# Local transformer stage: the score block directly ahead of the first mixture on TensorE, the row maxima behind the last rotation on VectorE

## The chip, the cores and the metric

The kernel runs on one core of one Trainium2 chip. The metric is the device time of one execution in microseconds (us); lower is better. The engines are TensorE (PE, with its weight loads as PEld), VectorE (DVE), ScalarE (ACT), GpSimd (POOL) and SyncE (SP), which only issues transfers here.

## The reference, cut to what matters

The whole network is four pairs of an attention branch `s` and a gate branch `g`, each joined by `x = x + s * silu(g)`. The change touches one branch only, the first gate: a local transformer of six layers over 16 sequences of 256 tokens with 16 heads of 64.

```python
def attn_layer(x, Wqkv, qs, ksc, Wo):
    q, k, v = (sh(t) for t in jnp.split(x @ Wqkv, 3, -1))
    q, k = l2norm(q) * qs, l2norm(k) * ksc
    q = q * cos * scale + rotate_half(q) * sin * scale
    k = k * cos / scale + rotate_half(k) * sin / scale
    # windows of 32 queries see their own 32 keys and the 32 before
    sim = jnp.einsum('bhwie,bhwje->bhwij', bq, bk2) * QK_SCALE
    sim = jnp.where(mask, -jnp.finfo(sim.dtype).max, sim)
    out = jnp.einsum('bhwij,bhwje->bhwie', jax.nn.softmax(sim, -1), bv2)
    return out.reshape(b, n, INNER) @ Wo
for i in range(6):
    x = attn_layer(shift_tokens(x), ...) + x
    x = ffn_layer(shift_tokens(x), ...) + x     # layer norm, two products, gelu gate
```

## The kernel before

The stage works on 192 tiles (six layers of 32 tiles of 128 tokens). It is a software pipeline written out by hand: `for n in range(LAST_STEP)` stands in the program of every engine, and in step n an engine does for tile n, n-1, n-2, n-3 and n-4 what falls to it. Each engine runs its own instructions strictly in the order written; semaphores tie them together. So what matters is which block stands where in a step. `now(lag)` is true where tile n - lag exists.

TensorE's blocks in a step, in their order before the change, with the names used below:

- P0, q0, P1, q1, O0, k0, O1, k1, P2: `project(n, unit)` (L1123, 128x512, units 0 to 3), `turn_qk(n - 2, ...)` (L1131, four transposes each) and `project_out(n - 4, part)` (L1186, parts O0 to O3)
- p0: `turn_probs(n - 3, 0)` (L1159, four transposes)
- S: `scores(n - 2)`, the mask as eight small products (L1142) and 128 passes of 64x64 (L1150)
- P3, p1 (the second half of `turn_probs`), O2
- every fourth step `turn_rows` (L1215); in two steps of a layer `turn_values`
- M0: `mix(n - 3, 0)` (L1174), the first half of probabilities times values
- in a step that is a multiple of four `hidden` (L1224) between the next blocks; in odd steps `turn_x` (L1113)
- O3, then M1: `mix(n - 3, 1)`

The two mixtures share the PSUM banks `u_bank`. M1 may overwrite nothing that ScalarE has not copied out:

```python
def mix(i, piece):
    pe.wait_ge(sem["copied"], copied_at["p", i, 1])
    if piece == 1 or i >= 1:
        pe.wait_ge(sem["u_copied"], 4 * i + 2 * piece)
```

ScalarE's order in a step, which the change leaves alone, ends as follows. The exponentials of tile n-2 stand ahead of the copy of the first mixture of tile n-3:

```python
    square(n, 3)
    copy_turned("p", n - 3, 1)
    exps(n - 2, 0); exps(n - 2, 1)              # L1336, wait for "shifted"
    copy_rows(...)                              # every fourth step, L1365
    copy_mixed(n - 3, 0)                        # L1344, sets "u_copied"
    copy_x(...); gelu(..., 0); gelu(..., 1)     # in some steps
    copy_mixed(n - 3, 1)
```

VectorE rotates the four projected units (`rotate`, three instructions each: L1507, L1511 and the sum of squares L1515), and in `shift_scores(n - 2)` takes the row maxima of the scores (L1522, two instructions, wait for "scored") and subtracts them (L1527, two instructions, set "shifted"). In one step of four `measure_rows` stands between `rotate(n, 1)` and `rotate(n, 2)`. The next step begins with `sum_probs` (L1534). GpSimd adds and normalises what was rotated, and divides the probabilities by their sums.

Of the kernel before, what the change touches and what calls it, by code (L numbers as in the profile page):

```python
# [885 lines left out]
def local_transformer_stage(core):  # L886
# [10 lines left out]
    with ExitStack() as ctx:  # L897
# [43 lines left out]
        def group_at(n, lag):  # L941
            q = (n - lag) // GROUP
            return q if (n - lag) % GROUP == 0 and 0 <= q < GROUPS else None

        def starts(n, at):
            return n // NT if n % NT == at and n < TILES else None
# [50 lines left out]
        def wait_turn_bank(pe, *key):  # L997
            k = turn_number[key]
            if k > 0:
                name, count = turn_free[k - 1]  # L1000
                pe.wait_ge(sem[name], count)

        def ring(*key):
            return ring_bank[ring_number[key] % 2]
# [7 lines left out]
        with nc.Block() as block:  # L1012
# [93 lines left out]
            def _(pe):  # L1106
# [28 lines left out]
                def scores(i):  # L1135
                    b, t = i // TPB, i % TPB
                    pe.wait_ge(sem["copied"], copied_at["k", i, 1])
                    if i >= 1:
                        pe.wait_ge(sem["shifted"], 2 * i)
                    for w in range(WPT):  # L1140
                        for h in range(2):
                            nc.tensor.matmul(score_bank[h][32 * w:32 * w + 32, :], core.pick[64 * h:64 * h + 64, :],  # L1142
                                             core.window_mask[64 * h:64 * h + 64, int(t == 0 and w == 0), :], start=True, stop=False,
                                             skip_group_check=True)
                    for j in range(PAIRS):
                        for w in range(WPT):
                            at = WINDOW * (WPT * t + w)
                            for h in range(2):
                                rows_h = slice(64 * h, 64 * h + 64)
                                last = nc.tensor.matmul(score_bank[h][32 * w:32 * w + 32, 64 * j:64 * j + 64],  # L1150
                                                        qt[rows_h, i % 2, j, 32 * w:32 * w + 32], kt[rows_h, b % 2, j, at:at + 2 * WINDOW],
                                                        start=False, stop=True, skip_group_check=True)
                    last.then_inc(sem["scored"], 1)
# [37 lines left out]
                def turn_values(l, half):  # L1191
                    pe.wait_ge(wvo_in, 32 * (l + 1))
                    wait_turn_bank(pe, "v", l, half)
                    for j in range(4):
                        at = (4 * half + j) * P
                        last = nc.tensor.transpose(turn_bank[:, j * P:(j + 1) * P], wv[:, at:at + P], core.ident[:, :])
                    last.then_inc(sem["turned"], 1)
# [41 lines left out]
                for n in range(LAST_STEP):  # L1239
                    now = lambda lag: 0 <= n - lag < TILES  # L1240
                    if now(0):
                        project(n, 0)
                    if now(2):
                        turn_qk(n - 2, "q", 0)
                    if now(0):
                        project(n, 1)
                    if now(2):
                        turn_qk(n - 2, "q", 1)
                    if now(4):
                        project_out(n - 4, 0)  # L1250
                    if now(2):
                        turn_qk(n - 2, "k", 0)
                    if now(4):
                        project_out(n - 4, 1)
                    if now(2):
                        turn_qk(n - 2, "k", 1)
                    if now(0):
                        project(n, 2)
                    if now(3):
                        turn_probs(n - 3, 0)  # L1260
                    if now(2):
                        scores(n - 2)
                    if now(0):
                        project(n, 3)
                    if now(3):
                        turn_probs(n - 3, 1)
                    if now(4):
                        project_out(n - 4, 2)
                    if group_at(n, 11) is not None:
                        turn_rows(group_at(n, 11))  # L1270
                    for half in range(2):
                        if starts(n, 1 + half) is not None:
                            turn_values(n // NT, half)
                    if now(3):
                        mix(n - 3, 0)
                    if group_at(n, 12) is not None:
                        hidden(group_at(n, 12), 0)
                    if n % 2 == 1 and n + 1 < TILES:
                        turn_x((n + 1) // 2)
                    if now(4):  # L1280
                        project_out(n - 4, 3)
                    if group_at(n, 12) is not None:
                        hidden(group_at(n, 12), 1)
                    if now(3):
                        mix(n - 3, 1)
                    if starts(n, 3) is not None:
                        multiply_weights(n // NT)
                    if group_at(n, 12) is not None:
                        hidden(group_at(n, 12), 2)
                    if group_at(n, 13) is not None:  # L1290
                        project_hidden(group_at(n, 13))
# [203 lines left out]
            def _(dve):  # L1495
                def rotate(i, unit):
                    g, t, which = UNITS * i + unit, i % TPB, unit // 2
                    if i % NT == 0 and unit % 2 == 0:
                        dve.wait_ge(rope_in[which], 16 * (i // NT + 1))
                    dve.wait_ge(sem["squared"], g + 1)  # L1500
                    if i >= 3:
                        wait_turned(dve, "qk"[which], i - 3, unit % 2)
                    if g >= 2:
                        dve.wait_ge(sem["added"], g - 1)
                    src = ring("p", i, unit)
                    cos = rope[:, which, t, 0, :].rearrange("p (a d) -> p a d", a=1).to_broadcast([P, 8, DH])
                    nc.vector.tensor_tensor(a[:, g % (3 * UNITS), :].rearrange("p (h d) -> p h d", d=DH), src.rearrange("p (h d) -> p h d", d=DH),  # L1507
                                            cos, ALU.mult)
                    halves = src.rearrange("p (h s d) -> p h s d", s=2, d=32)[:, :, ::-1, :]
                    sin = rope[:, which, t, 1, :].rearrange("p (a s d) -> p a s d", a=1, s=2).to_broadcast([P, 8, 2, 32])  # L1510
                    nc.vector.tensor_tensor(b_[:, g % 2, :].rearrange("p (h s d) -> p h s d", s=2, d=32), halves, sin,  # L1511
                                            ALU.mult).then_inc(sem["rotated"], 1)
                    if i >= 2 and unit == 0:
                        dve.wait_ge(sem["rn_ready"], i - 1)
                    nc.vector.tensor_reduce(n2[:, i % 2, 8 * unit:8 * unit + 8], sq[:, g % 2, :].rearrange("p (h d) -> p h d", d=DH), AX.X,  # L1515
                                            ALU.add).then_inc(sem["summed"], 1)
# [74 lines left out]
                for n in range(LAST_STEP):  # L1591
                    now = lambda lag: 0 <= n - lag < TILES
                    if now(3):
                        sum_probs(n - 3)
                    if now(5):
                        store(n - 5)
                    if group_at(n, 11) is not None:
                        normalise_rows_of(group_at(n, 11))
                    if now(0):
                        rotate(n, 0)  # L1600
                        rotate(n, 1)
                    if group_at(n, 9) is not None:
                        measure_rows(group_at(n, 9))
                    if now(0):
                        rotate(n, 2)
                    if now(2):
                        shift_scores(n - 2)
                    if now(0):
                        rotate(n, 3)
                    if group_at(n, 12) is not None:  # L1610
                        gate_hidden(group_at(n, 12))
                    if group_at(n, 13) is not None:
                        store_group(group_at(n, 13))
# [1286 lines left out]
```

## Time and profile before

| | |
|---|---|
| time, median of three runs | 5806.92 us (5806.7 to 5816.7) |
| time of the profiled execution | 5807.41 us |
| span of the profile | 5805.6 us |
| busy over the whole span | PE 83%, DVE 66%, PEld 58%, ACT 49%, POOL 44% |
| instructions | 144393 |
| busiest lines of the changed stage | POOL L1435 976.7 us, PE L1123 828.0 us, PE L1186 823.6 us |

The profiled time and the span differ by 1.8 us, the part outside the first and last instruction. The stage in question lies between about 219 and 3616 us of the span and takes well over half of it; the rest of the program is the same in both kernels. "Idle before, releaser" says how long an engine stood still ahead of a group and whose work ended that.

### The profile page before, as it was taken

Reading aid. Unit: us, or ns where it says so; the run is one execution under the profiler, and the core shown is the slowest. Engines: PE = TensorE matmul, PEld = TensorE weight load, DVE = VectorE, ACT = ScalarE, POOL = GpSimd, SP = SyncE. Lnnn points to the kernel's source line nnn. Section 1 sums busy time; section 2 is a strip of 40 time slices with the busy share of each in tenths; the row PEclk is TensorE's granted clock in tenths of the full one; section 3 lists DMA queues with packets and bytes.
Section 4 is the critical chain, followed back from the end, with each engine's and each line's share of the span. In section 5 each row is a group of like instructions: output and inputs, shape, how many; then the busy total and the mean of one; then the engine's idle time right before and its main releaser. Section 6 shows DMA issues by size and latency. Waiting matters only on the chain. (4 is left out here: it accounts for less than half of the span.)

```text
span 5805.6 us, 144393 instructions
## 1 busy us (share of the span) xinstructions
PE 4827.4 (83%) x57263; PEld 3362.5 (58%) x57263; DVE 3834.8 (66%) x9149; ACT 2866.4 (49%) x6252; POOL 2569.4 (44%) x3065
## 2 busy tenths in 40 slices
PE   7699999999999999999999998533689996067874
PEld 3366666666666666666666666323556664045653
DVE  7677777777777777777777775666367777633421
ACT  2266665666666666666666655200256664322331
POOL 4476666766777677667766765012200000000000
PEclk9899999999999999999999999765889998587987
DMA  0211111111111111111111100011100000001001
GB/s 20 67 31 24 25 33 35 24 25 39 31 24 33 31 28 24 33 34 27 24 33 23 26 20 13 21 41 55 31 18 2 2 2 3 20 5 27 25 21 39
DMA packets 312161, 150.56 MB, mean 26 GB/s; under 512 B 146143, under 2 KB 301003, under 8 KB 311243
## 3 DMA queue, kind: packets, MB, share of 16 engines
q1 hardware_dynamic: 309451, 137.20, 9.8%
q8 instruction: 457, 7.49, 0.5%
q0 software_dynamic: 2048, 4.20, 0.3%
q14 instruction: 205, 1.68, 0.1%
HBM read 101.10 MB, written 27.41 MB: 22 GB/s over the span
## 5 line engine op out<-in xcount | busy, mean ns | idle before, releaser
L1435 POOL TENSOR_TENSOR loc_a<-loc_a,loc_b 128x512 f32<-128x512 f32 x768 | 976.7, 1274 | 231.6 <-DVE loc_b L1511 231.0
L1123 PE MATMUL psum<-loc_wqk,loc_xt 128*128 128x512 f32 x1536 | 828.0, 621 | 19.0 <-issue 8.3
L1186 PE MATMUL psum<-loc_m,xn_rows 128*128 128x128 f32 x6144 | 823.6, 277 | 3.9 <-DVE y_rows L1543 2.6
L1307 ACT ACTIVATE loc_sq<-psum 128x512 f32<-128x512 f32 x768 | 455.1, 593 | 680.6 <-PE psum L1123 680.0
L1460 POOL TENSOR_TENSOR loc_a<-loc_a,loc_rn 128x512 f32<-128x512 f32 x768 | 785.4, 1045 | 0.1
L1186 PEld LDWEIGHTS psum<-loc_m,xn_rows 128*128 128x128 f32 x6144 | 754.1, 193 | 45.6 <-issue 42.6
L1507 DVE TENSOR_TENSOR loc_a<-psum,loc_rope 128x512 f32<-128x512 f32 x768 | 523.4, 681 | 334.8 <-ACT loc_sq L1307 322.5
L1467 POOL TENSOR_TENSOR xn_cols<-xn_cols,loc_rec 128x512 f32<-128x512 f32 x384 | 394.5, 1048 | 687.2 <-DVE loc_rec L1538 687.1
L1344 ACT COPY xn_rows<-psum 128x512 f32<-128x512 f32 x768 | 411.7, 588 | 221.6 <-PE psum L1174 217.6
L1511 DVE TENSOR_TENSOR loc_b<-psum,loc_rope 128x512 f32<-128x512 f32 x768 | 520.7, 678 | 0.0
L1515 DVE TENSOR_REDUCE loc_n<-loc_sq 128x8 f32<-128x512 f32 x768 | 517.1, 673 | 0.0
L1131 PEld LDWEIGHTS psum<-ident,loc_a 128*128 128x128 f32 x3072 | 338.9, 141 | 275.1 <-issue 262.3
L1131 PE MATMUL psum<-ident,loc_a 128*128 128x128 f32 x3072 | 478.1, 278 | 13.4 <-ACT loc_qt L1325 7.2
L1174 PE MATMUL psum<-xn_cols,loc_x 64*128 64x256 f32 x3072 | 437.8, 402 | 19.9 <-ACT xn_rows L1344 19.2
L1325 ACT COPY loc_kt<-psum 128x512 f32<-128x512 f32 x384 | 224.7, 585 | 312.5 <-PE psum L1131 312.5
L1150 PE MATMUL psum<-loc_kt,loc_qt 64*32 64x64 f32 x24576 | 293.1, 225 | 72.7 <-issue 72.6
L1174 PEld LDWEIGHTS psum<-xn_cols,loc_x 64*128 64x128 f32 x3072 | 273.4, 187 | 115.5 <-issue 80.0
L1150 PEld LDWEIGHTS psum<-loc_kt,loc_qt 64*32 64x32 f32 x24576 | 281.9, 105 | 88.5 <-issue 78.2
L364 POOL TENSOR_TENSOR s_rows<-s_rows,l2a_gamma 128x1024 f32<-128x1024 f32 x2 | 4.9, 2445 | 717.5 <-DVE s_rows L293 717.5
L1159 PEld LDWEIGHTS psum<-ident,xn_cols 128*128 128x128 f32 x1536 | 177.8, 141 | 238.8 <-issue 238.6
L1224 PE MATMUL psum<-x_rows,loc_w 128*128 128x512 f32 (+1 forms) x576 | 287.8, 623 | 18.3 <-ACT x_rows L1375 17.4
L1123 PEld LDWEIGHTS psum<-loc_wqk,loc_xt 128*128 128x128 f32 x1536 | 232.3, 190 | 113.1 <-issue 52.2
(365 smaller groups left out, 8819.5 us busy)
## 6 DMA issues: line engine op xcount, KB each, us to landing
loc_x<-loc_shifted SPq DMA_DIRECT2D x192, 256.0 KB, 4.0
loc_shifted<-y_rows SPq DMA_DIRECT2D x144, 64.0 KB
loc_wqk<-in_L_ffn_Wqkv SPq DMA_DIRECT2D x24, 256.0 KB, 3.7
x_rows<-y_rows SPq DMA_DIRECT2D x96, 64.0 KB
x_rows<-y_rows SPq DMA_DIRECT2D x96, 63.5 KB
moe_w<-in_L_ffn_W SPq DMA_DIRECT2D x16, 256.0 KB, 4.6
l3a_qk<-l3a_rot SPq DMA_DIRECT2D x16, 256.0 KB, 2.1
grp_w<-in_L_ffn_W SPq DMA_DIRECT2D x16, 256.0 KB, 2.8
```

The lines of the kernel that those rows point to most:

```text
L1123: nc.tensor.matmul(ring("p", i, unit), xt[:, b % 2, t * P:(t + 1) * P], wqk[:, unit * 512:(unit + 1) * 512], start=True, stop=True).then_i ...
L1131: last = nc.tensor.transpose(turn_bank[:, j * P:(j + 1) * P], a[:, (UNITS * i + unit) % (3 * UNITS), j * P:(j + 1) * P], core.ident[:, :])
L1150: last = nc.tensor.matmul(score_bank[h][32 * w:32 * w + 32, 64 * j:64 * j + 64], qt[rows_h, i % 2, j, 32 * w:32 * w + 32], kt[rows_h, b % ...
L1174: last = nc.tensor.matmul(u_bank[h][:, 256 * v:256 * v + 256], x2[rows_h, b % 3, WPT * t + w, :], pt[rows_h, i % 2, :, 32 * w:32 * w + 32] ...
L1186: last = nc.tensor.matmul(y_bank[:, 0:P], u[:, i % 2, h // 2, h % 2, :], m[:, h, :], start=(h == 0), stop=(h == HEADS - 1))
L1307: nc.scalar.activation(sq[:, g % 2, :], ring("p", i, unit), ACT.Square).then_inc(sem["squared"], 1)
L1344: nc.scalar.copy(to, u_bank[h].rearrange("p (w j q) -> p w j q", w=2, j=PAIRS)).then_inc(sem["u_copied"], 1)
L1435: nc.gpsimd.tensor_tensor(part, part, b_[:, g % 2, :], ALU.add).then_inc(sem["added"], 1)
L1460: nc.gpsimd.tensor_tensor(part, part, rn[:, i % 2, 8 * unit:8 * unit + 8].rearrange("p (h e) -> p h e", e=1).to_broadcast([P, 8, DH]), ALU ...
L1507: nc.vector.tensor_tensor(a[:, g % (3 * UNITS), :].rearrange("p (h d) -> p h d", d=DH), src.rearrange("p (h d) -> p h d", d=DH), cos, ALU. ...
L1511: nc.vector.tensor_tensor(b_[:, g % 2, :].rearrange("p (h s d) -> p h s d", s=2, d=32), halves, sin, ALU.mult).then_inc(sem["rotated"], 1)
L1515: nc.vector.tensor_reduce(n2[:, i % 2, 8 * unit:8 * unit + 8], sq[:, g % 2, :].rearrange("p (h d) -> p h d", d=DH), AX.X, ALU.add).then_in ...
```

## The change

On TensorE, `scores(n - 2)` moves from its place between p0 and P3 to a place behind P3, p1, O2 and the two occasional turns, directly ahead of M0. On VectorE, `shift_scores(n - 2)` moves from ahead of `rotate(n, 3)` to behind it. No instruction is added or removed, and ScalarE, GpSimd and SyncE keep their order.

```diff
@@ TensorE @@
                         turn_probs(n - 3, 0)
-                    if now(2):
-                        scores(n - 2)
                     if now(0):
                         project(n, 3)
...
                         if starts(n, 1 + half) is not None:
                             turn_values(n // NT, half)
+                    if now(2):
+                        scores(n - 2)
                     if now(3):
                         mix(n - 3, 0)
@@ VectorE @@
                     if now(0):
                         rotate(n, 2)
+                        rotate(n, 3)
                     if now(2):
                         shift_scores(n - 2)
-                    if now(0):
-                        rotate(n, 3)
```

TensorE's blocks from p0 to M1 in a plain step of the steady state (p0 is the first L1159 row, S the rows L1142 and L1150, P3 is L1123, M0 and M1 are L1174), before:

```order
L1159 MATMUL psum<-ident,xn_cols 128x128 x4
L1142 MATMUL psum<-loc_window_mask,loc_pick 32x512 x8
L1150 MATMUL psum<-loc_kt,loc_qt 32x64 x64
L1123 MATMUL psum<-loc_wqk,loc_xt 128x512
L1159 MATMUL psum<-ident,xn_cols 128x128 x4
L1186 MATMUL psum<-loc_m,xn_rows 128x128 x4
L1174 MATMUL psum<-xn_cols,loc_x 128x256 x4
L1186 MATMUL psum<-loc_m,xn_rows 128x128 x4
L1174 MATMUL psum<-xn_cols,loc_x 128x256 x4
```

The same blocks on TensorE in the changed kernel:

```order
L1159 MATMUL psum<-ident,xn_cols 128x128 x4
L1123 MATMUL psum<-loc_wqk,loc_xt 128x512
L1159 MATMUL psum<-ident,xn_cols 128x128 x4
L1186 MATMUL psum<-loc_m,xn_rows 128x128 x4
L1142 MATMUL psum<-loc_window_mask,loc_pick 32x512 x8
L1150 MATMUL psum<-loc_kt,loc_qt 32x64 x64
L1174 MATMUL psum<-xn_cols,loc_x 128x256 x4
L1186 MATMUL psum<-loc_m,xn_rows 128x128 x4
L1174 MATMUL psum<-xn_cols,loc_x 128x256 x4
```

S went down past three blocks; between S and M1 there were five blocks, and now there are two.

VectorE in the same step, from the third rotation to the sums of the next step, before:

```order
L1507 TENSOR_TENSOR loc_a<-psum,loc_rope 128x512
L1511 TENSOR_TENSOR loc_b<-psum,loc_rope 128x512
L1515 TENSOR_REDUCE loc_n<-loc_sq 128x8
L1522 TENSOR_REDUCE loc_top<-psum 128x8 x2
L1527 TENSOR_TENSOR xn_cols<-psum,loc_top 128x8x64 x2
L1507 TENSOR_TENSOR loc_a<-psum,loc_rope 128x512
L1511 TENSOR_TENSOR loc_b<-psum,loc_rope 128x512
L1515 TENSOR_REDUCE loc_n<-loc_sq 128x8
L1534 TENSOR_REDUCE loc_total<-xn_cols 128x8 x2
```

And VectorE in the changed kernel, at the same place:

```order
L1507 TENSOR_TENSOR loc_a<-psum,loc_rope 128x512
L1511 TENSOR_TENSOR loc_b<-psum,loc_rope 128x512
L1515 TENSOR_REDUCE loc_n<-loc_sq 128x8
L1507 TENSOR_TENSOR loc_a<-psum,loc_rope 128x512
L1511 TENSOR_TENSOR loc_b<-psum,loc_rope 128x512
L1515 TENSOR_REDUCE loc_n<-loc_sq 128x8
L1522 TENSOR_REDUCE loc_top<-psum 128x8 x2
L1527 TENSOR_TENSOR xn_cols<-psum,loc_top 128x8x64 x2
L1534 TENSOR_REDUCE loc_total<-xn_cols 128x8 x2
```

The maxima and the subtraction (L1522, L1527) stand one rotation later, directly ahead of the sums of the next step.

## Rows read from the trace of the kernel before

**Rows 1.** Busy time in one stretch of the stage; us, PE, PEld, DVE, ACT, POOL, PEclk, DMA:

```profile
core 0: us, PE busy (x) PEld busy (x) DVE busy (x) ACT busy (x) POOL busy (x), PEclk, DMA share, GB/s
2000.00:3000.00 1000.00, 964.01 (x13141) 683.34 (x13139) 751.21 (x1394) 616.18 (x1182) 707.52 (x866) 1.00 0.13 30
```

**Rows 2.** TensorE's waits, 600 to 3400 us; us in total, times, longest:

```profile
PE psum L1150 <- issue: 56.0, 39, 2.1
PE psum L1174 <- ACT xn_rows L1344: 14.9, 64, 0.3
```

**Rows 3.** Timeline of TensorE, plain step, p0 to M1; start, us, operation:

```profile
2004.82 0.63 PE L1159 MATMUL psum<-ident,xn_cols 128*128 128x128 f32 x4
2005.38 0.41 PE L1142 MATMUL psum<-loc_window_mask,loc_pick 64*32 64x512 bf16 x8
2005.60 1.46 PE L1150 MATMUL psum<-loc_kt,loc_qt 64*32 64x64 f32 x128
2006.99 1.13 PE L1123 MATMUL psum<-loc_wqk,loc_xt 128*128 128x512 f32 x2
2007.95 0.60 PE L1159 MATMUL psum<-ident,xn_cols 128*128 128x128 f32 x4
2008.39 1.06 PE L1186 MATMUL psum<-loc_m,xn_rows 128*128 128x128 f32 x8
2009.38 1.13 PE L1174 MATMUL psum<-xn_cols,loc_x 64*128 64x256 f32 x8
2010.44 1.16 PE L1186 MATMUL psum<-loc_m,xn_rows 128*128 128x128 f32 x8
2011.78 1.14 PE L1174 MATMUL psum<-xn_cols,loc_x 64*128 64x256 f32 x8 [0.18 <-ACT xn_rows L1344]
```

**Rows 4.** Timeline of VectorE and ScalarE, the same step:

```profile
2007.37 1.28 DVE L1522 TENSOR_REDUCE loc_top<-psum 128x8 f32<-128x512 f32 x2
...
2009.28 1.23 ACT L1336 ACTIVATE xn_cols<-xn_cols 128x512 f32<-128x512 f32 x2
...
2009.76 0.68 DVE L1507 TENSOR_TENSOR loc_a<-psum,loc_rope 128x512 f32<-128x512 f32 x1
...
2010.56 1.07 ACT L1344 COPY xn_rows<-psum 128x512 f32<-128x512 f32 x2
...
2011.55 1.27 DVE L1534 TENSOR_REDUCE loc_total<-xn_cols 128x8 f32<-128x512 f32 x2
```

**Rows 5.** Timeline of TensorE in a step with turned rows (L1215):

```profile
2023.96 0.63 PE L1215 MATMUL psum<-ident,loc_rows 128*128 128x128 f32 x4
2024.52 1.13 PE L1174 MATMUL psum<-xn_cols,loc_x 64*128 64x256 f32 x8
2025.91 0.41 PE L1113 MATMUL psum<-ident,y_rows 128*128 128x128 f32 x2 [0.26 <-ACT x_rows L1365]
```

**Rows 6.** Timeline of VectorE in a step with measured rows:

```profile
2127.83 1.27 DVE L1522 TENSOR_REDUCE loc_top<-psum 128x8 f32<-128x512 f32 x2
```

**Rows 7.** Timeline of TensorE in a step with hidden products (L1224):

```profile
2113.27 2.01 PE L1224 MATMUL psum<-x_rows,loc_w 128*128 128x512 f32 x4 [0.37 <-ACT x_rows L1375]
```

**Rows 8.** Timeline of TensorE around three stalls in the score block:

```profile
519.82 0.24 PE L1150 MATMUL psum<-loc_kt,loc_qt 64*32 64x64 f32 x1 [1.84 <-issue]
...
905.19 0.45 PE L1150 MATMUL psum<-loc_kt,loc_qt 64*32 64x64 f32 x29 [2.05 <-issue]
...
1228.42 0.34 PE L1150 MATMUL psum<-loc_kt,loc_qt 64*32 64x64 f32 x13 [1.86 <-issue]
1228.69 1.13 PE L1123 MATMUL psum<-loc_wqk,loc_xt 128*128 128x512 f32 x2
...
1235.08 1.14 PE L1174 MATMUL psum<-xn_cols,loc_x 64*128 64x256 f32 x8 [0.18 <-ACT xn_rows L1344]
```

**Rows 9.** Busy time and PEclk in the stretches behind those three stalls:

```profile
520.00:523.40 3.40, 3.40 (x23) 2.41 (x22) 3.30 (x6) 2.12 (x4) 2.72 (x3) 1.00 0.03 7
...
905.80:909.00 3.20, 3.20 (x10) 2.06 (x10) 3.20 (x6) 1.16 (x3) 0.45 (x1) 0.50 0.02 5
1230.10:1233.30 3.20, 3.20 (x16) 2.80 (x16) 3.20 (x7) 1.96 (x4) 2.02 (x3) 0.50 0.01 3
```

## The prediction

> **What bounds the kernel now.** I read the busy time of the stage first, then TensorE's waits, then the timeline of one step on three engines. In a thousand microseconds of the stage TensorE is busy for 964, at a granted clock of 1.00 (2.4 GHz), while VectorE, ScalarE and GpSimd have 25% to 38% to spare [rows 1]. So TensorE's stream is the bound: what makes it stand still is paid, unless it stands still later anyway. Its waits are few. The largest is "issue" inside the score block S, 39 times, 56.0 us; the next is the second mixture M1 on ScalarE's copies of the first one, 14.9 us in 64 steps, at most 0.3 us each [rows 2].
>
> That second entry is small but decides the case. In the plain step M1 starts at 2011.78 with a wait whose releaser is the copy L1344 [rows 3], and the copy ran from 2010.56 for 1.07, to 2011.63 [rows 4]. So M1 starts 0.15 behind the end of the copy: it has no slack against it. What holds the copy? ScalarE's two exponentials start at 2009.28 and take 1.23, to 2010.51, and the copy stands 0.05 behind them; M0 itself ends at 2009.38 + 1.13 = 2010.51 as well [rows 3, 4]. Both releases fall together: the reader should see a chain with zero slack that runs S, maxima (2007.37), exponentials (2009.28), copy (2010.56), M1 (2011.78). From the start of the maxima to M1 it takes 4.41 us [rows 3, 4]. The program's order puts the exponentials of tile n-2 ahead of the copy of tile n-3, so the copy inherits every delay of S, though its data have nothing to do with it.
>
> **What the change does, plain step.** S has 1.61 us to the next block and ends 1.68 behind its start (2005.60 + 1.46 - 2005.38). In the new order, from p0 at 2004.82: P3 may follow after 0.44 (as O2 follows p1, 2007.95 to 2008.39), at 2005.26; p1 after 0.96, at 2006.22; O2 at 2006.66; S after 0.99, at 2007.65; M0 after 1.61, at 2009.26 instead of 2009.38; S ends at 2009.33 [rows 3]. VectorE is no obstacle: the maxima's old place at 2007.37 goes to the fourth rotation, which takes 1.79 (2009.76 to 2011.55), so VectorE is free at 2009.16 [rows 4]. The maxima start on the end of S, about 2009.36, which is **1.99 us** later than before. With the same 4.41 us M1 starts at 2013.77, against 2011.78. TensorE has only O3 to hide that: M0 takes 1.06 to the next block, O3 starts at 2010.32 and ends 1.16 later, at 2011.48 [rows 3]. TensorE then stands still for **2.29 us** in every plain step.
>
> Nothing later gives that back. TensorE's next waits are small [rows 2], and P0, q0 and the rest follow M1 back to back. The fourth rotation is earlier, but TensorE did not wait for it. GpSimd gets the sums' reciprocals later by less than TensorE is delayed. The 0.12 us by which M0 is earlier is lost in the wait.
>
> **The other steps, four kinds in turn.**
> - Turned rows: S now also stands behind L1215, which takes 0.56 to the next block [rows 5]. `turn_x` (L1113) waits for ScalarE's L1365, which stands behind the exponentials, already 0.26 now [rows 5]. Everything moves by 1.99 + 0.56 = 2.55 us.
> - Measured rows: VectorE was late, with the maxima at 2127.83 [rows 6] directly behind its third rotation; one rotation more makes it +1.79 us, and S is ready by then.
> - Hidden products: the second hidden block waits for a gelu (L1375), 0.37 now [rows 7], and the gelus stand behind the same copy of M0; +1.99 us.
> - Plain: +1.99 us.
>
> The mean is 2.08 us. 191 steps have both an S and a mixture (192 tiles, one step apart), so the wait costs 397 us. In 12 steps (two a layer) `turn_values` is put ahead of S too, at the same 0.56: 7 us. Together **404 us**. I bound it by 1.9 and 2.25 us a step, 363 to 430 us.
>
> **The clock.** A stall of TensorE can cost more than its length. The stalls inside S are the nearest rows [rows 8]. Behind the one of 2.05 us and the one of 1.86 us the granted clock is 0.50 (1.2 GHz); behind the one of 1.84 us it stays 1.00 [rows 9]. In the second of them P3 to M1 takes 1235.08 - 1228.69 = 6.39 us [rows 8] where the plain step takes 2011.78 - 2006.99 = 4.79 [rows 3]: a fall costs 1.60 us on the path. The new gaps of 2.3 us and more are longer than each of these, and they come in every step. By these rows alone all would be followed by a fall (1.60 x 191 = 306 us); that equal stalls near 1.85 us go either way says that chance has a part, and heavy blocks, not S, stand beside the new gap. I take 0.7, and 0.4 and 1.0 as ends: 0.7 x 1.60 x 191 = **214 us**, between 122 and 306.
>
> The Trainium skill speaks against this term: "TensorE: Matmul & The Clock Gate", section "Why this matters for your kernels", warns only of gaps longer than the ones worked out here. By it the clock would hold and the sum would be 6211. The rows behind the stalls contradict it, so it is a rival only.
>
> **Sum.** 5807.4 (the profiled execution's own time, 0.5 above the median of the runs) + 404 + 214 = 6425 us.
>
> **The rivals.**
> - The wait without the falls. For it: busy blocks on both sides of the gap, and one stall of 1.84 us that was harmless [rows 9]. Against it: two shorter gaps with a fall. 5807 + 404 = 6211 us. Chance 0.08.
> - The stalls inside S go. The 56.0 us of "issue" in 2800 us [rows 2] may be TensorE outrunning the supply of its instructions, and with a pause in each step the supply could keep up. Over the 3400 us of the stage 68 us would be saved: 6357 us. Against it: S itself runs as fast as before. Chance 0.10.
> - The low clock keeps itself up: a fall on every step and half again as many more in the steps with longer gaps. 404 + 2 x 306 = 1016, 6823 us at its worst, from 6560 on. Chance 0.06.
> - Not slower. If M0's own end, and not the exponentials, set ScalarE's copy, M1 would keep its place: M0 even starts 0.12 us earlier (2009.26), giving 191 x 0.12 = 23 us, 5784 us. The two releases do coincide at 2010.51. It decides at maxima that start no later than 2007.37; but S cannot have ended by then in the new order, and ScalarE's order is fixed. Chance 0.02.
> - My forecast, wait and falls: 0.74.
>
> **How the numbers follow.** The predicted time is that of the forecast, 6425. Its own ends are 5807 + 363 + 122 = 6292 and 5807 + 430 + 306 = 6543. The range 6300 to 6545 holds it and the rival without stalls, and leaves out the other three, 0.16, and little more. Faster by over 0.2% (about what a measurement of this kernel can tell from no change) is the last rival, 0.02; within 0.2% would need a near-exact cancellation, 0.01; slower 0.97.
>
> **What the profile after would show.** TensorE's waits: L1174 on ScalarE L1344 as the first entry, some 2.3 us at a time in plain steps, where it was 0.3 at most, and L1113 on L1365 near 2.9 us in the steps with turned rows. The timeline: maxima directly behind the end of S, 4.41 us from maxima to M1. The stage's granted clock below 1.00: with 0.7 falls a step some 0.94, if each lasts a little over the 3.2 us shown at 0.50 [rows 9] in a step of some 20 us. A granted clock of 1.00 would refute the second term; M1 waits of under 1 us would refute the first. VectorE's and ScalarE's busy times should not change. The prediction goes wrong if the exponentials start before S ends plus 1.9 us, or if the falls come less often than four in ten steps.

## The result, and the profile after

The changed kernel takes 6368.71 us (median of four runs, 6363.59 to 6391.32), the kernel before 5811.81 us beside it (5806.7 to 5817.54). The ratio is 1.0965, 95% interval 1.0946 to 1.0984: slower by a tenth. The profiled execution took 6364.08 us with a span of 6362.3 us.

From the page of the changed kernel, busy time and TensorE's granted clock in 40 slices:

```profile
PE 4997.7 (79%) x57229; PEld 3461.3 (54%) x57263; DVE 3871.3 (61%) x9149; ACT 2874.0 (45%) x6252; POOL 2561.5 (40%) x3065
...
PEclk9899999999999999999999999986588999676987
```

VectorE, ScalarE and GpSimd are busy for as long as before, within 37 us. TensorE is busy for 170 us more (4827.4 before) with the same work: part of its work ran slower. The stage alone shows it, in the columns of [rows 1], before and after:

```profile
281.00:3600.00 3319.00, 3176.27 (x43068) 2251.24 (x43074) 2455.77 (x4557) 2030.12 (x3893) 2315.38 (x2831) 1.00 0.12 28
```

```profile
280.00:4147.00 3867.00, 3350.19 (x43017) 2348.47 (x43016) 2487.61 (x4544) 2034.60 (x3889) 2305.06 (x2828) 0.94 0.10 24
```

With all but the same instructions TensorE is busy for 174 us more and idle for 374 us more (517 against 143), together 548 of the 557 us. A mean of 0.94 between 1.0 and 0.5 is (1 - 0.94) x 2 x 3867 = some 460 us at the low clock. TensorE's waits in the stage, in the form of [rows 2], before:

```profile
PE psum L1150 <- issue: 71.5, 49, 2.1
PE psum L1174 <- ACT xn_rows L1344: 18.1, 78, 0.7
PE psum L1224 <- ACT x_rows L1375: 17.4, 46, 0.9
...
PE psum L1113 <- ACT x_rows L1365: 7.2, 28, 0.5
```

And after:

```profile
PE psum L1174 <- ACT xn_rows L1344: 199.9, 93, 2.8
PE psum L1113 <- ACT x_rows L1365: 128.6, 45, 3.1
PE psum L1224 <- ACT x_rows L1375: 107.5, 46, 2.4
PE psum L1150 <- issue: 46.3, 60, 2.1
```

The second mixture's wait for the copy of the first is now at the top, and the two waits of the other step kinds, for ScalarE's instructions behind the exponentials, follow. Together the three are 436 us, where they were 43. The stalls inside the score block went the other way, from 71.5 us in the whole stage to 46.3.

A plain step of the changed kernel on TensorE, from p0 to the block behind M1, to be laid beside [rows 3]:

```profile
2535.68 0.63 PE L1159 MATMUL psum<-ident,xn_cols 128*128 128x128 f32 x4
2536.15 1.02 PE L1123 MATMUL psum<-loc_wqk,loc_xt 128*128 128x512 f32 x2
...
2538.53 0.41 PE L1142 MATMUL psum<-loc_window_mask,loc_pick 64*32 64x512 bf16 x8
2538.75 1.46 PE L1150 MATMUL psum<-loc_kt,loc_qt 64*32 64x64 f32 x128
2540.14 1.13 PE L1174 MATMUL psum<-xn_cols,loc_x 64*128 64x256 f32 x8
2541.20 1.16 PE L1186 MATMUL psum<-loc_m,xn_rows 128*128 128x128 f32 x8
2544.62 2.08 PE L1174 MATMUL psum<-xn_cols,loc_x 64*128 64x256 f32 x8 [2.26 <-ACT xn_rows L1344]
2546.63 1.72 PE L1123 MATMUL psum<-loc_wqk,loc_xt 128*128 128x512 f32 x2
```

VectorE in the same step, from the fourth rotation to the subtraction, beside [rows 4]:

```profile
2538.58 0.69 DVE L1507 TENSOR_TENSOR loc_a<-psum,loc_rope 128x512 f32<-128x512 f32 x1 [0.26 <-POOL loc_a L1435]
...
2540.38 1.28 DVE L1522 TENSOR_REDUCE loc_top<-psum 128x8 f32<-128x512 f32 x2
```

And ScalarE, the exponentials and the copy behind them:

```profile
2542.29 1.23 ACT L1336 ACTIVATE xn_cols<-xn_cols 128x512 f32<-128x512 f32 x2 [3.96 <-DVE xn_cols L1527]
2543.43 1.05 ACT L1344 COPY xn_rows<-psum 128x512 f32<-128x512 f32 x2
```

From p0 the score block starts at 2.85 us (worked out: 2.83), M0 at 4.46 (4.44), the maxima at 4.70 (4.54) and M1 at 8.94 (8.95). M0 ended at 2541.27, and the copy of its result begins at 2543.43: its data lay ready for 2.16 us while ScalarE waited for maxima of another tile. TensorE stands still for 2.26 us (2.29). Behind the pause M1 takes 2.01 us to the next block, where [rows 3] has M0 with 1.06. The clock in the stretches ahead of, behind and after that pause:

```profile
2520.00:2544.40 24.40, 20.15 (x312) 15.51 (x294) 16.64 (x30) 11.85 (x24) 16.49 (x20) 1.00 0.08 18
2544.60:2547.80 3.20, 3.18 (x10) 1.91 (x11) 2.72 (x5) 1.06 (x2) 2.04 (x2) 0.50 0.00 0
2548.00:2560.00 12.00, 11.88 (x203) 8.66 (x201) 8.49 (x14) 5.84 (x12) 9.81 (x12) 1.00 0.22 47
```

The granted clock falls to 1.2 GHz as the pause ends and is back at 2.4 GHz some three microseconds later, after M1 and most of P0 ran slowly. Not every pause has this behind it: counted in the trace between the first and the last score block, 49 of the 106 pauses of 2.1 to 2.4 us were followed by a fall, and 33 of the 44 of 2.8 to 3.2 us. In the step with turned rows the pause is longer, 2.93 us ahead of L1113 (0.26 in [rows 5]):

```profile
2323.84 0.41 PE L1113 MATMUL psum<-ident,y_rows 128*128 128x128 f32 x2 [2.93 <-ACT x_rows L1365]
```

### The profile page after: what moved, and what is told of

Same layout as the page of the kernel before. It is cut to its first block and busy times, and to the rows that moved or that the text cites. A ratio compares the mean times of both kernels' runs of the same rounds, so it can differ in the third digit from the quotient of the medians.

```text
span 6362.3 us, 144359 instructions
## 1 busy us (share of the span) xinstructions
PE 4997.7 (79%) x57229; PEld 3461.3 (54%) x57263; DVE 3871.3 (61%) x9149; ACT 2874.0 (45%) x6252; POOL 2561.5 (40%) x3065
## 5 line engine op out<-in xcount | busy, mean ns | idle before, releaser
L1435 POOL TENSOR_TENSOR loc_a<-loc_a,loc_b 128x512 f32<-128x512 f32 x768 | 970.5, 1276 | 45.3 <-DVE loc_b L1511 45.2
L1123 PE MATMUL psum<-loc_wqk,loc_xt 128*128 128x512 f32 x1536 | 859.5, 643 | 10.3 <-ACT loc_m L1356 4.6
L1186 PE MATMUL psum<-loc_m,xn_rows 128*128 128x128 f32 x6144 | 850.8, 283 | 5.0 <-DVE y_rows L1543 2.6
L1186 PEld LDWEIGHTS psum<-loc_m,xn_rows 128*128 128x128 f32 x6144 | 780.1, 198 | 47.1 <-issue 44.3
L1174 PE MATMUL psum<-xn_cols,loc_x 64*128 64x256 f32 x3072 | 499.6, 445 | 210.8 <-ACT xn_rows L1344 205.1
L1336 ACT ACTIVATE xn_cols<-xn_cols 128x512 f32<-128x512 f32 x384 | 235.6, 630 | 839.8 <-DVE xn_cols L1527 839.8
L1511 DVE TENSOR_TENSOR loc_b<-psum,loc_rope 128x512 f32<-128x512 f32 x768 | 522.4, 680 | 0.0
L1131 PEld LDWEIGHTS psum<-ident,loc_a 128*128 128x128 f32 x3072 | 352.5, 145 | 305.9 <-issue 291.9
L1131 PE MATMUL psum<-ident,loc_a 128*128 128x128 f32 x3072 | 488.1, 283 | 14.7 <-ACT loc_qt L1325 7.1
L1174 PEld LDWEIGHTS psum<-xn_cols,loc_x 64*128 64x128 f32 x3072 | 307.0, 209 | 324.2 <-issue 284.7
L1224 PE MATMUL psum<-x_rows,loc_w 128*128 128x512 f32 (+1 forms) x576 | 312.9, 670 | 108.4 <-ACT x_rows L1375 107.5
L1576 DVE SCALAR_TENSOR_TENSOR x_rows<-psum,loc_b,x_rows 128x512 f32<-128x512 f32 x144 | 107.9, 750 | 372.7 <-PE psum L1224 199.9
L1150 PE MATMUL psum<-loc_kt,loc_qt 64*32 64x64 f32 x24576 | 294.3, 224 | 48.0 <-issue 48.0
L1150 PEld LDWEIGHTS psum<-loc_kt,loc_qt 64*32 64x32 f32 x24576 | 281.5, 105 | 67.4 <-issue 57.1
L1522 DVE TENSOR_REDUCE loc_top<-psum 128x8 f32<-128x512 f32 x384 | 246.7, 684 | 115.3 <-PE psum L1150 110.4
```

Of the source, the lines that this page charges most:

```text
L1123: nc.tensor.matmul(ring("p", i, unit), xt[:, b % 2, t * P:(t + 1) * P], wqk[:, unit * 512:(unit + 1) * 512], start=True, stop=True).then_i ...
L1174: last = nc.tensor.matmul(u_bank[h][:, 256 * v:256 * v + 256], x2[rows_h, b % 3, WPT * t + w, :], pt[rows_h, i % 2, :, 32 * w:32 * w + 32] ...
L1186: last = nc.tensor.matmul(y_bank[:, 0:P], u[:, i % 2, h // 2, h % 2, :], m[:, h, :], start=(h == 0), stop=(h == HEADS - 1))
L1435: nc.gpsimd.tensor_tensor(part, part, b_[:, g % 2, :], ALU.add).then_inc(sem["added"], 1)
```

## The experiments

The account to be tested has two terms: the exponentials ahead of the copy on ScalarE carry every delay of the score block into M1 (wait), and the pauses lower TensorE's clock (falls). Rivals: VectorE's new order is what costs; the wait belongs to the data; the low clock costs nothing on the path. All ratios are to the kernel before on the same chip, whose medians there were 5823 to 5826 us; it was 5811.81 us beside the changed kernel, so differences of some ten microseconds between versions timed on different chips say little.

**E1, the TensorE half alone.** The score block in its new place, VectorE as before.

```diff
                         rotate(n, 2)
-                        rotate(n, 3)
                     if now(2):
                         shift_scores(n - 2)
+                    if now(0):
+                        rotate(n, 3)
```

> The TensorE half of the change alone: the score block directly ahead of the first mixture, VectorE's maxima in their old place ahead of the fourth rotation. Theory (the maxima start on the end of the score block, the exponentials and the copy of the first mixture follow it, and the second mixture waits for that copy): as slow as the changed kernel, 6345 to 6375 us, since VectorE's order was no obstacle in the plain step; only in the one step of four with measured rows may the maxima start some 0.3 us earlier, 48 times, 14 us. Rival (the slowdown comes from VectorE's new order): near 5810 us.

Measured: 6343.7 us, ratio 1.0903 (1.0873 to 1.0933). The TensorE half makes nearly the whole loss: 520 us over the kernel before beside it, where the whole change has 557. Some 36 us are left for the rotation of 1.79 us that the whole change puts ahead of the maxima, more than the 14 expected, but little beside the 342 us that 191 rotations take. E1's first waits differ from the changed kernel's in one:

```profile
PE psum L1174 <- ACT xn_rows L1344: 189.7, 93, 2.8
PE psum L1113 <- ACT x_rows L1365: 127.4, 45, 3.1
PE psum L1224 <- DVE loc_b L1511: 74.6, 45, 1.7
```

With the rotation behind the maxima, the hidden products wait for the fourth rotation (loc_b, L1511) to free their bank.

**E2, the VectorE half alone.** TensorE as before, the maxima behind the fourth rotation.

```diff
                         rotate(n, 2)
+                        rotate(n, 3)
                     if now(2):
                         shift_scores(n - 2)
-                    if now(0):
-                        rotate(n, 3)
```

> The VectorE half alone: TensorE in its old order, the maxima behind the fourth rotation. Theory: the rotation (1.79 us) stands between the third rotation and the maxima, the copy and the second mixture are late by the same 1.79 us in every step, 191 x 1.79 = 342 us, and the gaps make some falls of the clock, 100 to 200 us: 6250 to 6350 us. Rival (the maxima have slack, since their place in the new kernel costs nothing): under 5900 us.

Measured: 6726.78 us, ratio 1.1552 (1.1529 to 1.1576), far above what I expected, and worse than the whole change. VectorE in a plain step of E2, from the third rotation's last instruction to the maxima:

```profile
2488.80 0.68 DVE L1515 TENSOR_REDUCE loc_n<-loc_sq 128x8 f32<-128x512 f32 x1
2490.80 0.69 DVE L1507 TENSOR_TENSOR loc_a<-psum,loc_rope 128x512 f32<-128x512 f32 x1 [1.32 <-ACT loc_sq L1307]
...
2492.61 1.27 DVE L1522 TENSOR_REDUCE loc_top<-psum 128x8 f32<-128x512 f32 x2
```

TensorE in the same step, P3 and M1:

```profile
2489.01 1.13 PE L1123 MATMUL psum<-loc_wqk,loc_xt 128*128 128x512 f32 x2
...
2496.84 1.22 PE L1174 MATMUL psum<-xn_cols,loc_x 64*128 64x256 f32 x4 [3.22 <-ACT xn_rows L1344]
```

The fourth rotation needs P3 and its square, and in the old TensorE order P3 stands behind the score block. VectorE idles 1.32 us for it, and the maxima, whose scores have long been there, idle behind it: they start at 2492.61, 3.1 us behind the end of the third rotation at 2489.48, where in the step of [rows 4] they followed it at once. Counted from the start of the score block (L1142 at 2487.40) they are at 5.21 us instead of 1.99, so 3.22 us late and not 1.79. TensorE's busy time grew by 347 us (5174.8 against 4827.4), where I had 100 to 200 for the clock. 3.22 x 191 + 347 = 962 is close to the 939 us between the two spans (6744.3 and 5805.6). The miss was mine, since I had taken the rotation's duration and not what it waits for.

**E3, the copy ahead of the exponentials.** The changed kernel with one edit on ScalarE.

```diff
-                    if now(2):
-                        exps(n - 2, 0)
-                        exps(n - 2, 1)
...
                     if now(3):
                         copy_mixed(n - 3, 0)
+                    if now(2):
+                        exps(n - 2, 0)
+                        exps(n - 2, 1)
```

> The changed kernel with one more edit, on ScalarE: the copy of the first mixture stands ahead of the exponentials instead of behind them. Theory: the second mixture then waits for nothing but the first mixture and its copy; the 2.0 to 2.5 us go away in plain, measured and turned-rows steps, and the clock stays at 1.00. In the steps with hidden products the gelus now stand behind 1.2 us of exponentials, so those keep some 1.1 us of loss, 48 times, 53 us, while the steps with turned rows win some 0.4 us, 20 us: 5800 to 5860 us. Rival (the wait belongs to the data, or the low clock would stay without the gap): over 6100 us.

Measured: 5836.64 us, ratio 1.0023 (1.0011 to 1.0034). The loss is gone but for 13 us. E3's first waits of TensorE:

```profile
PE psum L1224 <- ACT x_rows L1375: 65.1, 46, 1.4
PE psum L1150 <- issue: 58.5, 66, 2.1
PE psum L1123 <- ACT loc_xt L1300: 17.9, 39, 0.5
...
PE psum L1174 <- ACT xn_rows L1344: 8.5, 48, 0.2
```

M1's wait fell from 199.9 to 8.5 us. What is left is where it was expected, in the gelus of the hidden steps (L1375), which now stand behind the exponentials. The copy of x (L1300), made in odd steps, is a new, small wait of the projections.

**E4, the pause filled.** The changed kernel with products whose results are thrown away, where TensorE would stand still.

```diff
+                def fill(n, count):
+                    if n % 4:
+                        pe.wait_ge(sem["rotated"], UNITS * (n + 1))
+                    to = ring("p", n, 3) if n % 4 else turn_bank
+                    for _ in range(count):
+                        nc.tensor.matmul(to[:, 0:P], core.ident[:, :], core.ident[:, :], start=True, stop=True,
+                                         skip_group_check=True)
...
+                    if now(3) and now(0) and n % 4 == 3:
+                        fill(n, 10)
                     if n % 2 == 1 and n + 1 < TILES:
                         turn_x((n + 1) // 2)
                     if now(4):
                         project_out(n - 4, 3)
+                    if now(3) and now(0) and n % 4 != 3:
+                        fill(n, 6 if n % 4 == 1 else 8)
```

> The changed kernel with products of the identity with itself (128x128, results thrown away, nothing of the computation left out) in TensorE's pause: 8 behind the third part of the output product, 6 in steps with measured rows, 10 ahead of the turn of x in steps with turned rows. They take about as long as the pause, so the wait itself stays. Theory with two terms (wait 404 us, falls of the clock the rest): the granted clock of the stage goes back to nearly 1.00 and the time falls by the clock's part, 150 to 210 us, to 6160 to 6230 us. Rival (the low clock costs nothing on the path, the wait is all): 6360 us or more, since the products can only add.

Measured: 6197.11 us, ratio 1.0645 (1.0623 to 1.0667). Some 1500 products more, and 172 us less than the changed kernel. E4's stage:

```profile
280.00:3975.00 3695.00, 3499.42 (x46010) 2569.39 (x46011) 2483.67 (x4543) 2027.40 (x3883) 2306.77 (x2828) 1.00 0.11 25
```

The granted clock is 1.00 again. The loss against the kernel before beside it is 374 us (6197.11 - 5823.3) instead of 557, so the falls make some 183 us (172 by the medians as they stand, which come from two chips). The 374 us are an upper bound of the wait, since the products may add a little of their own. The split of the stage of the changed kernel says the same without any filling: 174 us more busy, 374 us more idle.

**E5, a small dose.** The score block down past P3 alone, VectorE as before.

```diff
-                    if now(2):
-                        scores(n - 2)
                     if now(0):
                         project(n, 3)
+                    if now(2):
+                        scores(n - 2)
                     if now(3):
                         turn_probs(n - 3, 1)
```

> A small dose: the score block goes down past P3 alone (p0, P3, scores, p1, O2, M0), the maxima stay ahead of the fourth rotation. Theory (no slack at all between the maxima and the second mixture): the score block ends 0.96 - 0.1 us later, the maxima start 0.6 us later in plain, hidden and turned-rows steps and 0.1 us later in steps with measured rows, mean 0.47; 191 x 0.47 = 90 us over the kernel before on the same chip, ratio 1.013 to 1.018, and gaps of under 1 us leave the clock at 1.00. Rival (there is some slack, and only a long delay costs): ratio under 1.003.

Measured: 5860.34 us, ratio 1.0053 (1.0035 to 1.0072), 31 to 34 us. There is a loss at the smallest step down, but a third of the one I expected. E5's waits and stage:

```profile
PE psum L1174 <- ACT xn_rows L1344: 53.2, 93, 0.8
PE psum L1150 <- issue: 46.6, 60, 1.6
PE psum L1113 <- ACT x_rows L1365: 42.7, 45, 1.2
...
277.00:3637.00 3360.00, 3170.18 (x43016) 2221.06 (x43015) 2472.79 (x4544) 2041.93 (x3889) 2314.18 (x2828) 1.00 0.12 28
```

The waits are short and the clock stays at 1.00. M1's wait grew from 18.1 us to 53.2 and that of `turn_x` (L1113) from 7.2 to 42.7, together by 71 us, while the stalls in the score block fell from 71.5 to 46.6 us and took back a third of it. Two things keep the loss below the 90 us expected: this, and a slack of 0.14 us in the plain step, which is read out further down. (The spans of the two profiles are 52.7 us apart, 5858.3 and 5805.6, the medians only 34, since they come from different chips.)

**E6, P3 first and the maxima late.** E5 with the maxima behind the fourth rotation, to test the reading of E2.

```diff
# on top of E5
                         rotate(n, 2)
+                        rotate(n, 3)
                     if now(2):
                         shift_scores(n - 2)
-                    if now(0):
-                        rotate(n, 3)
```

> As e5, with the maxima behind the fourth rotation. This is the VectorE half in an order in which P3 stands ahead of the score block, so that the fourth rotation does not wait for P3. If the large loss of the VectorE half alone (1.155) came from P3 standing behind the score block, which put the maxima 3.2 us late instead of 1.79, then here they are 1.8 us late: 191 x 1.8 = 344 us and 100 to 200 us for the clock, ratio 1.075 to 1.095. Rival (VectorE's order costs 3 us by itself): ratio over 1.14.

Measured: 6184.35 us, ratio 1.0612 (1.0585 to 1.064). With P3 ahead, the same VectorE order costs 324 us (against E5, 5860.34) where it cost 903 in E2. That confirms the reading of E2. The size was missed: 358 us over the kernel before, where I had 444 to 544. The stage shows in which term, beside the row of the kernel before:

```profile
279.00:3969.00 3690.00, 3288.66 (x43017) 2297.57 (x43016) 2474.99 (x4544) 2044.40 (x3889) 2303.48 (x2828) 0.96 0.11 25
```

TensorE is busy for 112 us more, within the 100 to 200 expected for the clock, and idle for 259 us more, where I had 344. So the wait was too large in my sum: 1.35 us a step and not 1.8. Why less of the delay arrives here was not tested.

**E7, the score block ahead of the occasional turns.** The changed kernel with `scores` above `turn_rows` and `turn_values`.

```diff
+                    if now(2):
+                        scores(n - 2)
                     if group_at(n, 11) is not None:
                         turn_rows(group_at(n, 11))
...
-                    if now(2):
-                        scores(n - 2)
                     if now(3):
                         mix(n - 3, 0)
```

> The changed kernel with the score block ahead of the turned rows and the turned values instead of behind them. Theory: the 0.56 us go away in 48 + 12 steps, 34 us, and with shorter gaps there some 10 to 25 us of the clock's part: 45 to 60 us less than the changed kernel, ratio 1.085 to 1.090 to the kernel before. Rival (in these steps ScalarE's rows copy sets the end): ratio 1.094 or more.

Measured: 6324.14 us, ratio 1.0843 (1.0811 to 1.0875). That is 498 us over the kernel before beside it, 59 us less than the changed kernel's 557, at the upper end of the 45 to 60 expected. In its stage TensorE is idle for 487 us (517 in the changed kernel) and busy for 3325.9 us (3350.2): 30 us of wait, where 34 were expected, and 24 us of clock.

**E8 and E9, can the new order win?** E8 is the kernel before with ScalarE's edit in all but the hidden steps. E9 has E8's ScalarE, and TensorE and VectorE in the changed order except in hidden steps.

```diff
# ScalarE, E8 and E9
-                    if now(2):
+                    if now(2) and group_at(n, 12) is not None:
                         exps(n - 2, 0)
                         exps(n - 2, 1)
...
                     if n % 2 == 1 and n + 1 < TILES:
                         copy_x((n + 1) // 2)
+                    if now(2) and group_at(n, 12) is None:
+                        exps(n - 2, 0)
+                        exps(n - 2, 1)
# TensorE, E9 alone, ahead of P3 and ahead of M0; VectorE alike
+                    if now(2) and group_at(n, 12) is not None:
                         scores(n - 2)
...
+                    if now(2) and group_at(n, 12) is None:
+                        scores(n - 2)
```

> Control for the next run. The kernel before with ScalarE's edit alone: except in steps with hidden products, the exponentials stand behind the copy of the first mixture and the copy of x. TensorE and VectorE as before. Theory: in plain steps the first mixture and the exponentials end together, so nothing is won; in measured-rows steps up to 0.3 us, in turned-rows steps 0.1 us: 10 to 20 us, ratio 0.996 to 0.999. Rival (the exponentials, now 1.8 us later in odd steps, delay the next step): over 1.002.

Measured: 5838.39 us, ratio 1.0017 (1.0003 to 1.0032). The 10 to 20 us were not won; it is slightly slower. In its profile the clock fell 20 times between the first and the last score block, in the kernel before 7 times: 78 us at the low clock against 31.

> The best order that the runs so far point to: in the steps with hidden products TensorE, VectorE and ScalarE keep the order of the kernel before; in all others TensorE and VectorE have the changed order, and ScalarE does the exponentials behind the copy of the first mixture and the copy of x. From e3 (plain -0.11 us, measured-rows -0.42 us a step, and the turned-rows step freed of its wait for the copy of x, some -0.4 us): 48 x 0.9 = 45 us less than the kernel before, ratio 0.990 to 0.996. Rival (what was won in e3's steps is given back where the two orders meet, or the exponentials, later by 0.7 us in odd steps, hold the next step): ratio 0.998 or more.

Measured: 5804.09 us, ratio 0.9964 (0.995 to 0.9978). It is the one version that beats the kernel before, by 21 us, less than half of the 45 I expected. E9's waits of TensorE show what is new:

```profile
PE psum L1150 <- issue: 65.6, 58, 2.0
PE psum L1131 <- ACT loc_qt L1327: 18.0, 40, 1.5
PE psum L1224 <- ACT x_rows L1377: 17.4, 46, 0.9
```

The transposes of q in the next step now wait for ScalarE's copies (L1131 on loc_qt, 18.0 us). E8 has the same wait, 17.6 us in 43 steps, so it comes with the later exponentials. E8 and E9 differ in the order on TensorE and VectorE alone, so the gain of E9 comes with that order: the move that cost 557 us gains a little in these steps once ScalarE no longer couples it to M1. By what way is less clear than I expected. From the first to the last score block E8's profile takes 3388.1 us with 78 us at the low clock and 80.8 us of stalls in the score block, and E9's takes 3344.7 us with 41 and 67.3 us. That puts the difference in the stalls and the falls behind them, and not in an earlier start of M0. Against the kernel before, the two profiles are only 4.5 us apart (5801.1 and 5805.6), and the 21 us of the medians are not located.

## Why the prediction was right

- **The bound and the chain.** Right. The chain from maxima to M1 read out of [rows 3] and [rows 4] decided the case. E3 removes the coupling and nearly all of the loss; E5 shows a loss from the first half microsecond on. "Zero slack" was a little too strict. In [rows 4] the copy starts 1.28 us behind the exponentials; in the changed kernel, where M0's result lies ready, it starts 1.14 us behind them (2542.29 to 2543.43). So in the plain step before it was M0 that released the copy, and the exponentials had 0.14 us to spare. The condition of the last rival was met, but it holds only for the first 0.14 us of a delay of 2 us.
- **The wait, 404 us.** Right in place and size. 2.26 us of pause in the plain step stand against 2.29, and 2.93 ahead of L1113 against the 2.9 forecast. The measured bound is 374 us (E4), and the idle time of the stage grew by 374. What the sum did not have is the shrinking of the stalls in the score block, which I had kept as a rival of its own at 68 us: it happened in part, 25 us, alongside the forecast and not instead of it. The rival's reason, that a pause in each step lets the supply keep up, does not hold as it stands: E2 has the longest pauses of all and the most stalls, 93.9 us (see the last section).
- **The fourth rotation as no obstacle.** Right in effect, for an incomplete reason. In the changed kernel it waits 0.26 us for GpSimd (L1435), so the maxima are 0.16 us later from p0 than worked out. In the plain step this costs nothing, because it is made up by the 0.14 us of slack at the copy. Over the stage the VectorE half costs some 36 us (E1 against the whole change). The same blind spot, a duration taken without its releasers, was costly in E2.
- **The falls, 214 us.** Right in mechanism, a little too high. E4 gives 172 to 183 us, and TensorE's busy time in the stage grew by 174. The granted clock of the stage is 0.94 as forecast, but it is made up otherwise: counted in the trace from the first to the last score block, the clock fell 111 times (7 in the kernel before), where 0.7 x 191 made 134, and 27 of the 111 slow stretches lasted twice as long as the others. The 175 us of busy time over 104 falls more is 1.7 us each, close to the 1.60 read from one step; what was too high is the number of falls. That 0.94 came out exactly is therefore in part luck.
- **The sum.** 6425 was forecast, 6364 profiled, 6369 the median. The excess of some 60 us is 30 to 40 of the falls and 25 of the stalls.
- **The rivals.** The wait without falls was refuted by the clock and by E4, and a low clock that keeps itself up by the 111 falls in 191 steps. "Not slower" was refuted as it stood: M0 is indeed earlier, but ScalarE's order decides. Its condition is what E3 and E9 then made true.

The advice in the Trainium skill's "TensorE: Matmul & The Clock Gate", section "Why this matters for your kernels", warns only of idle gaps of more than about 3 us; here a pause of 2.26 us was followed by 1.2 GHz, as were 49 of the 106 of its kind, and filling such pauses brought the clock back. The measurement decides.

## What to carry to other kernels

In a hand-written order, look at every engine for an instruction that stands behind another one whose input is late, though its own is ready: here ScalarE's copy behind the exponentials. Before a block is moved down on one engine, follow that coupling to where it comes back, and compare the delay with what is left to hide it; before an instruction is moved up, look at what it waits for and not only at how long it takes. A pause of 2 us and more repeated in each step was charged twice here, once as a wait and once in TensorE's clock (in E5, with waits on ScalarE of at most 1.2 us, the clock stayed at 1.00); products whose results are thrown away, put into the pause, tell the two apart.

## What the hardware showed that was not expected

- Extra work made the kernel faster: some 190 pauses filled with products of the identity took 172 us off (6368.71 to 6197.11, 183 when each is set against its own kernel before), with the stage's granted clock from 0.94 back to 1.00.
- The "issue" stalls inside the score block are not a fixed charge, and they go first of all by the place of the block, not by the pauses of TensorE: E2, with the longest pauses, has the most. The table has them for the whole stage; the last column counts those of over 1 us. What separates versions with the same place, up to 22 us, was not tested.

| run | place of the score block | stalls, us | of over 1 us |
|---|---|---|---|
| before | behind p0 | 71.5 | 48 |
| E8 | behind p0 | 76.2 | 48 |
| E2 | behind p0 | 93.9 | 57 |
| E9 | mixed | 65.6 | 35 |
| E5, E6 | behind P3 | 46.6, 56.4 | 12, 16 |
| E7 | behind O2 | 46.9 | 12 |
| changed, E1, E3, E4 | directly ahead of M0 | 46.3, 54.3, 58.5, 56.7 | 13, 21, 24, 20 |

- Each of the 48 long stalls of the kernel before ends 1.18 to 1.55 us behind the landing of a 16 KB transfer on the queue of instructions, and 2.15 to 2.81 us behind its start; in the changed kernel the 13 long stalls end 1.19 to 1.51 us behind such a landing. Such a transfer comes only every 9.6 us there (349 in 3354 us), so this is no coincidence, and I read these stalls as TensorE waiting for its instructions. Why the place of the score block changes their number was not tested.
- A longer pause was followed by a low clock more often: 49 of 106 pauses of 2.1 to 2.4 us in the changed kernel, 33 of 44 of 2.8 to 3.2 us.
